# First convolution on its own input, the other three composed: seven filter taps in four slots

## The reference, cut to what matters

```python
def _layer(x, style, w, b, mw, mb, typ):
    s = style @ mw.T + mb
    weight = SCALE * w * s[:, None, :, None]
    demod = lax.rsqrt(jnp.sum(weight * weight, axis=(2, 3)) + EPS)
    weight = weight * demod[:, :, None, None]
    if typ == 'same':
        out = jax.vmap(_conv_same)(x, weight) + b[None, :, None]
    elif typ == 'upsample':
        out = jax.vmap(_conv_up)(x, weight.transpose(0, 2, 1, 3)) + b[None, :, None]
        out = _blur(out, 2.0 * blur_k, (1, 1))
    elif typ == 'downsample':
        xb = _blur(x, blur_k, (2, 2))
        out = jax.vmap(_conv_down)(xb, weight) + b[None, :, None]
    return out
...
TYPES = ('same', 'upsample', 'same', 'downsample')
```

## Time and profile before

| | us |
|---|---|
| median of 3 runs (1483.17 to 1484.88) | 1484.66 |
| span of the profiled execution | 1481.5 |
| TensorE busy in it | 1457.1 |
| DVE busy | 992.7 |
| ACT busy | 719.4 |
| POOL busy | 465.1 |

### The profile page before, as it was taken

One profiled execution on the slowest core, in us unless ns is written; L12 is line 12 of the kernel. 1 busy time (PEld: TensorE's weight loads), 2 busy tenths in 40 slices (PEclk: granted clock), 3 DMA queues, 4 the chain that ended last, 5 costly groups with the idle time before them and its releaser, 6 DMA issues.

```text
span 1481.5 us, 28220 instructions
## 1 busy us (share of the span) xinstructions
PE 1457.1 (98%) x9619; PEld 1370.7 (93%) x9619; DVE 992.7 (67%) x2355; ACT 719.4 (49%) x1618; POOL 465.1 (31%) x542
## 2 busy tenths in 40 slices
PE   6999999999999999999989999999999999999999
PEld 4889898988988898889879999999999999999998
DVE  8766667766566655555676677677677677677674
ACT  5455445555544554455444445445454454454452
POOL 4133233323323332333313233233233233232230
PEclk9999999999999999999999999999999999999999
DMA  6443433443243234323533423423424424324322
GB/s 134 108 110 77 114 101 78 114 116 101 72 114 104 80 101 113 106 76 101 142 122 78 113 69 100 113 65 104 113 60 110 112 58 113 109 61 113 107 63 71
DMA packets 56635, 145.14 MB, mean 98 GB/s; under 512 B 19365, under 2 KB 21861, under 8 KB 56586
## 3 DMA queue, kind: packets, MB, share of 16 engines
q1 hardware_dynamic: 55928, 144.19, 36.2%
q10 hardware_dynamic: 658, 0.30, 0.1%
HBM read 110.92 MB, written 33.55 MB: 98 GB/s over the span
## 4 chain that ended last, share of the span: by engine, by line
PE 95%; DVE 3%; DMA 0%; issue 0%; SPq 0%; POOL 0%; ACT 0%; DVEq 0%; POOLq 0%; ACTq 0%
PE bank L1564 48%; PE bank L1416 13%; PE bank L1418 13%; PE bank L1417 13%; PE bank L1724 4%; PE bank L1596 1%; PE bank L1585 1%; PE bank L1629 1%; PE bank L1658 0%; DMA ends<-in_x_dram 0%; DVE win L1159 0%; DVE mtmp L1158 0%; PE bank L1741 0%; PE bank L1647 0%; DVE fw_l L1153 0%
## 5 line engine op out<-in xcount | busy, mean ns | idle before, releaser
L1564 PE MATMUL bank<-fw_h,ct_h 128*128 128x354 f32 (+2 forms) x1256 | 448.0, 357 | 0.8 <-DVE xout L1124 0.8
L1564 PE MATMUL bank<-fw_l,ct_h 128*128 128x354 f32 (+2 forms) x1256 | 445.1, 354 | 0.0
L1564 PE MATMUL bank<-fw_h,ct_l 128*128 128x354 f32 (+2 forms) x1256 | 443.2, 353 | 0.0
L414 POOL COPY conv_buf<-edge 128x4 f32 (+1 forms) x128 | 21.2, 193 | 848.9 <-DVE tw L1251 835.0
L1564 PEld LDWEIGHTS bank<-fw_h,ct_l 128*128 128x128 f32 x1256 | 236.1, 188 | 21.3
L1564 PEld LDWEIGHTS bank<-fw_h,ct_h 128*128 128x128 f32 x1256 | 236.7, 188 | 17.6 <-DVE ct_l L1275 0.9
L1564 PEld LDWEIGHTS bank<-fw_l,ct_h 128*128 128x128 f32 x1256 | 236.5, 188 | 15.5
L405 POOL TENSOR_TENSOR d_l<-d_f,d_h 128x512 fp32r<-128x512 f32 x128 | 154.8, 1209 | 102.4 <-ACT d_h L634 102.2
L1416 PE MATMUL bank<-d_h,tw 128*128 128x256 f32 x640 | 181.8, 284 | 0.3 <-DVE beta L974 0.3
L1418 PE MATMUL bank<-d_h,tw 128*128 128x256 f32 x640 | 180.5, 282 | 0.0
L1417 PE MATMUL bank<-d_l,tw 128*128 128x256 f32 x640 | 180.0, 281 | 0.0
(11 more groups left out here) (246 smaller groups left out, 3114.6 us busy)
## 6 DMA issues: line engine op xcount, KB each, us to landing
xraw<-in_x_dram SPq DMA_DIRECT2D x32, 512.0 KB, 6.6
xres<-in_x_dram SPq DMA_DIRECT2D x32, 512.0 KB, 4.2
x_dram<-xout SPq DMA_DIRECT2D x32, 512.0 KB, 2.9
xraw<-x_dram SPq DMA_DIRECT2D x32, 512.0 KB, 6.4
xres<-x_dram SPq DMA_DIRECT2D x32, 512.0 KB, 4.4
xraw<-in_x_dram SPq DMA_DIRECT2D x32, 511.5 KB, 8.0
xraw<-x_dram SPq DMA_DIRECT2D x32, 511.5 KB, 7.9
out_dram<-xout SPq DMA_DIRECT2D x31, 512.0 KB, 2.9
```

Source lines behind the costliest of these rows:

```text
L1564: last = mm(ffn_ps[e][:, 0:cols.stop - cols.start], ctf((ct_h, ct_h, ct_l)[part], k), (fw_h, fw_l, fw_h)[part][:, k, cols], start=k == beg ...
```

## The change

The first convolution is taken out of the composed filter. It runs on the input by itself, three taps by the same fast scheme, and the composed filter holds the other three convolutions: seven taps, laid in four slots (NSH = 4) and three sums, seven slots in all.

- ACT scales the loaded input into a new buffer `sig` (`x_scale`, 512 elements a half, every second one read). POOL's differences and low parts and ACT's rounding read `sig` (every second element) and not `xraw` (every fourth).
- `stage_mix` on TensorE replaces `stage_t`: per half three products groups (difference, difference, odd samples), nine products, with constant weights `w1_h`, `w1_l`. In `body` it stands where `stage_u` stood, and `stage_u` three products of the sequence product later.
- `mix_scaled` (ACT) and `mix_out` (DVE, two operations a half) join the result and write it back into `sig`. POOL then forms differences and low parts a second time (`mixed`), ACT rounds a second time (`y_high`), before the convolution.
- The taps are taken from `stage_u`'s result by copies (`f_high`, `f_low`) into `t_f`, which has its own memory now; `z_high`, `z_low` and the scaling in `t_low` are gone. The convolution has six taps per half, not eight.
- POOL no longer waits for the taps. SP waits for `x_scaled`, not `x_ready`. The opening and the change of layers are rearranged in the same manner.

```diff
-NSH = 5
+NSH = 4
...
                 def neighbours(j, ly=ly):
                     s = ly["s"]
-                    pool.wait_ge(s["x_load"], 32 * j + 32)
                     for h in range(2):
-                        m0, m1 = (xraw[:, h, at:at + L].rearrange("p (n e q) -> p e n q", e=2, q=2)[:, :, :, 0] for at in (0, 2))
-                        nc.gpsimd.tensor_tensor(d_f[h][:, :, :], m0, m1, ALU.subtract).then_inc(s["d_made"], 1)
+                        pool.wait_ge(s["x_scaled"], 2 * j + h + 1)
+                        differ(h).then_inc(s["d_made"], 1)
...
+                def mixed(j):
+                    for h in range(2):
+                        pool.wait_ge(s["y_made"], 2 * j + h + 1)
+                        differ(h).then_inc(s["d_made"], 1)
+                    for h in range(2):
+                        pool.wait_ge(s["x_hi"], halves(j, h, True))
+                        lows(h).then_inc(s["x_ready"], 1)
...
                 def body(j, last=False):
 
-                    pool.wait_ge(s["t_ready"], 2 * j + 2)
+                    mixed(j)
+                    pool.wait_ge(s["ct_acc"], 2 * j)
                     edges(j)
                     if not last:
-                        x_next(j)
+                        neighbours(j + 1)
+                        split_low(j + 1)
...
+                nc.scalar.activation(sig[:, h, 0:HL], xraw[:, h, 0:L:2], ACT.Copy,
+                                     scale=ly["s_all"][:, 0, bass.ds(2 * j + h, 1)]).then_inc(s["x_scaled"], 1)
...
-                    z_high(j)
+                    mix_scaled(j, 0)
+                    mix_scaled(j, 1)
+                    y_high(j, 0)
+                    f_high(j)
+                    y_high(j, 1)
                     t_high(j)
...
                     if ly["lora"]:
                         gate_exp(j - 1)
+                    x_take(j, 0, last)
+                    x_take(j, 1, last)
...
+                def mix_out(j, h):
+
+                    dve.wait_ge(s["p_scaled"], halves(j, h))
+                    dve.wait_ge(s["conv_acc"], halves(j, h))
+                    even = sig[:, h, 0:HL:2]
+                    stt(out=sig[:, h, 1:HL:2], in0=conv_ps[h][:, QL:2 * QL], scalar=neg1[:, bass.ds(2 * j + h, 1)],
+                        in1=even, op0=ALU.mult, op1=ALU.add)
+                    stt(out=even, in0=conv_ps[h][:, 0:QL], scalar=lam1[:, bass.ds(2 * j + h, 1)],
+                        in1=even, op0=ALU.mult, op1=ALU.add).then_inc(s["y_made"], 1)
...
                     if not v_done:
                         v_low(j)
+                    mix_out(j, 0)
+                    mix_out(j, 1)
                     if step is not None:
                         prep_behind_v(step)
-                    z_low(j)
+                    f_low(j)
                     t_low(j)
...
-                    for i, slot in enumerate((G0, G1, 4)):
-                        last = conv_tap(h, comp_ps[h][:, 0:QL], slot, o_h[h][:, i:i + QL], o_l[h][:, i:i + QL], i == 0, i == 2)
+                    for i, slot in enumerate((G0, G1)):
+                        last = conv_tap(h, comp_ps[h][:, 0:QL], slot, o_h[h][:, i:i + QL], o_l[h][:, i:i + QL], i == 0, i == 1)
...
                 def body(j, step=None):
                     stage_v(j)
                     ffn(ly, j - 1, 0, 9)
+                    stage_mix(j, 0)
+                    stage_mix(j, 1)
+                    ffn(ly, j - 1, 9, 12)
                     stage_u(j)
-                    ffn(ly, j - 1, 9, 19)
-                    stage_t(j)
-                    ffn(ly, j - 1, 19, 33)
+                    ffn(ly, j - 1, 12, 33)
                     stage_conv(j, 0)
                     stage_conv(j, 1)
                     ffn(ly, j - 1, 33, 39)
```

More of the change, by code:

```diff
@@ L1137, in _ @@
                         v.memset(tw[h][half(0), :, 0, 1, :].bitcast(F32), 0.0)
-                    v.memset(z_f[half(1), :, 3, :], 0.0)
+                    for h in range(2):
+                        v.memset(t_f[h][half(1), 3, :], 0.0)
                     link(v.memset(bb[:, :].bitcast(F32), 0.0))
@@ L1365, in _ @@
                     fw_low(10, 12)
[L1366 removed]
+                    f_low(1)
                     w2_low(ly, 2)
@@ L1686, in stage_u, with stage_mix, sums @@
                     last.then_inc(s["u_acc"], 1)
-                def stage_t(j):
-                    for h in range(2):
-                        pe.wait_ge(s["z_ready"], 2 * j + h + 1)
-                        for g in range(2):
-                            last = three(comp_ps[h][:, C * g:C * (g + 4)], w1_h[:, 2 * C * g:2 * C * g + P],
-                                         w1_l[:, 2 * C * g:2 * C * g + P], flat(z_h[:, h, :, :]), flat(z_l[:, h, :, :]),
-                                         g == 0, g == 1)
-                        last.then_inc(s["t_acc"], 1)
+                def stage_mix(j, h, first=False):
+                    pe.wait_ge(s["x_ready"], halves(j, h))
+                    if not first:
+                        pe.wait_ge(s["ct_ready"], 4 * j)
+                    elif ly["lora"]:
+                        pe.wait_ge(layers[0]["s"]["ct_ready"], 4 * NPAIR)
+                    w = [(w1_h[:, i * P:(i + 1) * P], w1_l[:, i * P:(i + 1) * P]) for i in range(3)]
+                    mid = slice(1, QL + 1)
+                    def sums():
+                        if not h:
+                            pe.wait_ge(s["v_ready"], 2 * j + 2)
+                        three(m_ps[h], *w[2], o_h[h][:, mid], o_l[h][:, mid], True, True).then_inc(s["p_acc"], 1)
+                    late = first and not ly["lora"]
+                    if not late:
+                        sums()
+                    three(conv_ps[h][:, 0:QL], *w[0], d_h[h][:, 0, mid], d_l[h][:, 0, mid], True, True)
+                    three(conv_ps[h][:, QL:2 * QL], *w[1], d_h[h][:, 1, mid], d_l[h][:, 1, mid], False, True).then_inc(s["conv_acc"], 1)
+                    if late:
+                        sums()
@@ L1845, in body_lora @@
                         stage_v(j)
+                    else:
+                        pe.wait_ge(s["f_act"], 2 * j + 2)
+                        pe.wait_ge(s["f_dve"], 2 * j + 2)
                     ffn(ly, j - 1, 0, 13)
+                    stage_mix(j, 0)
+                    stage_mix(j, 1)
+                    ffn(ly, j - 1, 13, 17)
                     if not composed:
                         stage_u(j)
-                    ffn(ly, j - 1, 13, 28)
-                    if not composed:
-                        stage_t(j)
-                    ffn(ly, j - 1, 28, 49)
+                    ffn(ly, j - 1, 17, 49)
                     stage_conv(j, 0)
```

282 lines of the change are left out of this document (161 added, 121 removed).

## The result

The changed kernel takes **1543.84 us** (median of 4 runs, 1543.27 to 1543.98), the kernel before 1484.77 in the same session: a ratio of 1.0399, with a 95% interval of 1.0384 to 1.0414. It is slower by 59 us. 1574 was forecast, with a range of 1473 to 1636: the side is right, the size off by 30 us.

The account below looks back on a forecast made before the run. TensorE, busy 98% of the span, was taken as the bound. On a base of 1484.66 us, 30 x 0.8 (layer 0), 30 x 1.85 (layer 1), 8 (preparation) and 2 (opening) gave +89.5: about 1574 us, range 1473 to 1636.

Parts of the forecast that it names:

- counted in turns: Before the convolution, DVE's six tap operations and POOL's four remaining ones alternate, each turn its row less 0.13 us.
- Rivals 1 and 2: Rival 1: DVE comes first at the port, no convolution wait for taps, 1454 us, chance 0.12; rival 2 has its own line.
- rival 2: At the shared port only DVE's copies are held up, additions and subtractions run on: 1473 us, chance 0.08.
- Rival 3: Lateness adds up through POOL's doubled work into the next `stage_mix`, 1605 us and up; waits could lower the clock; chance 0.08.
- TensorE's saving: Per pair, 54 of 60 products over 256 columns remain: 0.70 us saved if nothing waits.
- Layer 0, +0.8 a pair: Net loss per layer 0 pair: convolution wait 1.05 plus turn wait 0.45 less 0.70 saved, in us.
- the 1.05: Layer 0's convolution waits for the tap copy: 0.87 us late plus 0.2 us pick-up.
- The turn's 0.45: Layer 0's second half of `stage_turn` waits 0.45 us for output at 19.2, due at 18.9, with pick-up.
- The low end of the range: Low strided-read prices on ACT and POOL: 0 in layer 0, +1.2 us a pair in layer 1; low end 1517 us.
- Layer 1, +1.85: Loss per layer 1 pair: taps 0.75, gates' transposition 0.9 and turn 0.9 less 0.70 saved, in us.
- Preparation pairs, +8: Twenty layer 0 pairs with layer 1's preparation on DVE; about half meet POOL's differences, 0.8 us each: +8, 0 to 20.
- Opening and change of layers, +2 (-4 to +6): Outside the loops: a chain more and four pairs' saving less, +2 us, between -4 and +6.

Follow-up runs that it names:

- short_lows: Changed kernel with POOL's low parts of the mixed input cut to 8 of 256 columns from each layer's second pair (leaves work out): 1468.53 us.
- the best version without waits: Changed kernel with TensorE's convolutions and turns later, the opening's third bias first, and layer 1's `w2` low part behind both result halves: 1470.26 us.
- held_differences: Changed kernel with POOL's differences for the next pair in layer 1 held until DVE has finished the gates: 1530.36 us.
- bias_first: Changed kernel with the opening's third bias placed ahead of the edges' second step on DVE: 1540.75 us.
- opening_lows: bias_first with POOL's low parts of the first pair in layer 0's opening cut to 8 of 256 columns (leaves work out): 1536.46 us.

## Why the prediction was right, and where it was off

**Direction and mechanism held.** The port between DVE and POOL, counted in turns, decides; short_lows shows it by taking POOL's rows away. Rivals 1 and 2 fall: the wait for the taps exists, and additions and differences are stretched, not copies alone. The note of the Trainium skill, Advanced Engine Details and Errata, VectorE Performance Modes, from which rival 2 came, names two-port instructions; here plain fp32 additions and differences of two SBUF operands, 0.36 and 0.62 alone, took 0.78 and 1.01 on the mean. Rows with an operand in PSUM kept their length beside POOL: the two of 657.88 and 658.28 above, 0.48 and 0.47, lie beside its differences (656.71 to 658.76). Rival 3 falls in its main part: no wait is listed in front of `stage_mix` in the loops, and cover removes the lateness. Its remark on the clock came true in two places, told below.

**TensorE's saving**: 0.70 forecast, 0.65 in the late pairs of layer 0 in short_lows. In layer 1 the best version without waits has 21.80 for 22.31, 0.5.

**Layer 0, +0.8 a pair, measured 0.0.** The order of the turns came as written; the times ran ahead from its first entries. With 642.13 as zero: POOL's first low part ends at 8.54 (forecast 8.66), the additions at 9.58 (9.79), the first difference at 11.12 (11.34), the copy at 12.22 (12.63), and the convolution starts at 12.35, due at 11.85. So the 1.05 was 0.60: 0.50, and 0.10 in the wider gap behind the first product. The copy came 0.41 before its forecast, for three reasons. The strided prices in front of the turns were too high: POOL's differences took 1.06 (taken: 1.3), ACT's rounding of every second element 0.42 on the mean (taken: 0.55). POOL began 0.23 later than forecast and its first low part took a whole row, so that only 0.12 of this was left when that part ended. Another 0.16 came in the turns, mostly those of `o_l`. And 0.13 is a slip in the sum: each turn was to be its row less 0.13, but the last copy was counted in full (12.01 + 0.49 = 12.50). The turn's 0.45 did not appear: ACT starts the scaling of the next input at 655.88, 13.75 behind the pair's start, not 14.2, and the second half's output ends at 18.5, not 19.2. The low end of the range had the right prices: with them the text gave 0 in layer 0 and +1.2 in layer 1, measured 0.0 and +1.32. That the first agrees to the tenth is partly luck, as that sum holds the slip of 0.13 too. Taking the middle added 30 x 0.8 = 24 us in layer 0 and 30 x 0.53 = 16 in layer 1 that did not come. The sum at the low prices, about 1531 us, misses by 13, most of it in the opening.

The Trainium skill, SBUF — State Buffer, Specifications, had given the low price from its lines of 16 bytes; ACT's 0.42 against 0.41 for 256 in a row and 0.68 for every fourth element agrees with it.

**Layer 1, +1.85, measured +1.32.** By starts the convolution lost 0.2 (forecast 0.75), the transposition 0.7 and the turn about 0.95 (0.9 each), less a saving of 0.5. The gates behind the taps and beside POOL's differences were the right step; held_differences shows it. The step on the turn was right in size, but its reason was half: the second half's result stood behind `w2`'s low part as well as behind the gates.

**Preparation pairs, +8**: layer 0's +11.4 is +10.2 in these twenty pairs, +0.5 in the first pair and +0.75 in the last, since the others gained and lost nothing. The longest of them, 24.19 us where it was 21.13, holds the longest wait of the loops, 1.96 us, and 1.2 us of work behind it the clock fell. TensorE's timeline at the start of that convolution:

```profile
261.56 0.36 PE L1503 MATMUL bank<-o_h,tw 128*128 128x256 f32 x1 [1.96 <-DVE tw L1329]
```

The window behind it (length, TensorE's busy time and rows, granted clock, share and rate of transfers):

```profile
262.80:266.20 3.40, 3.40 (x18) 0.50 0.01 2
```

With 0.50 TensorE worked at 1.2 GHz for 3.4 us. From 262.72 to 266.25 its products over 256 columns came 0.21 apart and not 0.12, which cost some 1.5 us (an estimate: 17 spacings, 3.53 us for 2.04). In short_lows, without the wait, that pair took 20.50 and the clock stayed at 1.00.

**Opening and change of layers, +2 (-4 to +6), measured +10.9 with the end.** This step failed, outside its own bounds. "A chain more" left out two things: the third bias had moved behind the edges' step on DVE (3.1 us, bias_first), and POOL's low parts stood beside VectorE's tables (4.3 us, opening_lows). The same port that was priced in the loops was not looked for here. The clock fell there as well: 0.72 to 0.81 between 28 and 62 us, against 0.86 and then full in the kernel before. The prediction had read the clock from the page's forty slices; those of the changed kernel show one 8 among the nines, and only the shorter windows show the fall. TensorE was busy for 3.05 of the 10 us from 40 to 50. In the loops of the changed kernel the clock stayed at 1.00 but for the 3.4 us behind the wait of 1.96; the other waits for the taps (up to 1.60 us) and those of layer 1 (up to 0.77) left it there.

The errors partly cancelled, which is luck: +8.9 in the opening, the change of layers and the end, against -20.6 in layer 0 and -17.1 in layer 1.

## What to carry to other kernels

Before work is moved onto POOL, look at what DVE does in the same stretch: here rows that read and write SBUF alone took turns with POOL's, and a short DVE row on the critical chain then cost about as much as POOL's row (the gates' copy 1.04 for 0.18). A saving on the bound engine is worth what its longest feeding chain leaves; here it came back only when TensorE's order gave that chain more cover, and cover at one place is taken from the next. And price an unseen access pattern from both ends, then say what the sum is at each end; look for the known conflict in the opening too, not only in the loops.

## What the runs showed of the hardware beyond that

- POOL's difference over 512 elements that reads every second one (1.06 us) is shorter than its low part over 512 that reads neighbours (1.18 to 1.20 when nothing shares the port), though the first reads with a step and the second does not. The first writes fp32, the second fp32r.
- A blocked DVE row ended 0.48 to 0.49 us behind the POOL row before it, for a difference of 0.62 as for a copy of 0.62, both longer than 0.49: some 0.13 of the DVE row lies over the end of POOL's.
- A wait of 0.34 us in TensorE's rows cost 0.60 by the starts: the idle time is counted from a modelled end, and the first product behind it comes with a gap of 0.22 where 0.12 is the rule.
